# First loads on two DMA queues, and the layer norm of the first batches shared out among three engines, in a gated cross-attention kernel with an expert layer

## What is computed

```python
q = layernorm(x) @ Wq + bq                      # 8 x 256 x 256
k, v = ctx @ Wk + bk, ctx @ Wv + bv             # 8 x 120 x 256
x = x + tanh(g_xattn) * softmax(q @ k.T) / 16 @ v
h = layernorm(x)
e = argmax(h @ router_w.T)                      # one of 8 experts for each token
y = (silu(h @ gate_w[e].T) * (h @ up_w[e].T)) @ down_w[e].T   # inner width 704
out = x + tanh(g_ffn) * y
```

## Time and profile before

| | us |
|---|---|
| median of three runs | 236.29 |
| lowest and highest | 235.4, 236.63 |
| the profiled execution, its own time | 235.78 |
| its span in the profile | 233.9 |

### The profile page before, as it was taken

How to read it: one execution, slowest core, us unless ns; L and a number is a source line. 1 busy time by engine, 2 the same in 40 slices (tenths; PEclk the granted TensorE clock), 3 DMA queues, 4 the chain that set the end, 5 groups by cost and what they waited for, 6 DMA issues and landing times.

```text
span 233.9 us, 4473 instructions
## 1 busy us (share of the span) xinstructions
PE 199.9 (85%) x1187; PEld 171.1 (73%) x1187; DVE 132.8 (57%) x436; ACT 107.5 (46%) x217; POOL 133.0 (57%) x124
## 2 busy tenths in 40 slices
PE   0797699998774788999999999999999999999620
PEld 0655688896674667888887888888888887888510
DVE  0289689977669505636544636546546545556410
ACT  2233577776420145465339475267494304443200
POOL 3000009869273699329966989967989962331110
PEclk9999999999859559999999999999999999999985
DMA  4999211773910116641481093381011031110010
GB/s 83 369 382 383 98 48 46 245 271 116 372 36 0 55 38 244 213 152 45 144 326 28 1 353 115 137 323 49 1 49 44 1 93 24 49 46 4 1 45 0
DMA packets 11824, 29.41 MB, mean 126 GB/s; under 512 B 2222, under 2 KB 8241, under 8 KB 10770
## 3 DMA queue, kind: packets, MB, share of 16 engines
q1 hardware_dynamic: 6848, 21.70, 26.1%
q0 software_dynamic: 2064, 5.12, 7.3%
q10 hardware_dynamic: 2882, 2.24, 2.8%
HBM read 24.85 MB, written 4.72 MB: 126 GB/s over the span
## 4 chain that ended last, share of the span: by engine, by line
PE 72%; DVE 13%; issue 5%; DMA 4%; ACT 2%; SPq 1%; POOL 0%; ACTq 0%; POOLq 0%; DVEq 0%
PE ps L860 33%; PE ps L872 12%; PE ps L839 6%; PE ps L875 5%; DMA xin<-in_x 4%; PE ps L746 3%; PE ps L767 3%; DVE st L942 2%; PE ps L717 2%; PE ps L832 2%; PE ps L728 2%; PE ps L756 2%; PE ps L708 1%; PE ps L809 1%; DVE V L1067 1%
## 5 line engine op out<-in xcount | busy, mean ns | idle before, releaser
L860 PE MATMUL ps<-wgu,xhT 128*128 x360 | 83.2, 385 | 1.2 <-issue 1.2
L860 PEld LDWEIGHTS ps<-wgu,xhT 128*128 128x128 f32 x360 | 66.4, 192 | 12.4 <-issue 1.6
L872 PE MATMUL ps<-wd,hT 128*128 x120 | 42.9, 395 | 2.5 <-DVE hT L1112 2.4
L451 POOL DMA_INDIRECT xin<-x_rows,table x23 | 22.8, 990 | 31.7 <-DVE xin L1133 22.8
L386 POOL TENSOR_TENSOR wgu<-raw_gu,wgu (+1 forms) x12 | 38.6, 3252 | 0.1
L1120 DVE TENSOR_TENSOR A<-xin,ps 128x512 f32<-128x512 f32 (+1 forms) x40 | 20.5, 520 | 26.7 <-ACT xin L624 12.2
L409 POOL TENSOR_TENSOR wgu<-raw_gu,wgu 128x352 fp32r<-128x352 f32 x16 | 14.5, 945 | 34.7 <-ACT wgu L548 34.7
L624 ACT ACTIVATE xin<-ps 128x512 f32<-128x512 f32 (+1 forms) x40 | 18.4, 466 | 31.5 <-PE ps L860 27.8
L456 POOL DMA_INDIRECT out<-xin,table x20 | 20.3, 1016 | 19.7 <-DVE xin L1133 14.5
L618 ACT ACTIVATE hT<-ps 128x512 fp32r<-128x512 f32 x20 | 11.9, 593 | 35.3 <-PE ps L839 30.9
L875 PE MATMUL ps<-wd,hT 128*128 x100 | 28.0, 280 | 0.0
(11 more groups left out here) (148 smaller groups left out, 290.2 us busy)
## 6 DMA issues: line engine op xcount, KB each, us to landing
raw_gu<-in_Wgu SPq DMA_DIRECT2D x8, 1408.0 KB, 8.1
both<-in_Wd SPq DMA_DIRECT2D x8, 640.0 KB, 4.6
xin<-in_x SPq DMA_DIRECT2D x8, 256.0 KB, 8.0
x_rows<-x ACTq DMA_DIRECT2D x8, 256.0 KB, 4.2
both<-in_WdL SPq DMA_DIRECT2D x16, 64.0 KB, 4.7
both<-in_ctxT SPq DMA_DIRECT2D x1, 960.0 KB, 8.2
xin<-x_rows,table POOLq DMA_INDIRECT x23
out<-xin,table POOLq DMA_INDIRECT x20
```

The lines of the kernel that those rows point to most:

```text
L451: pool.indirect_dma_start(out=xg[:, j % SEATS, :], out_offset=None, in_=rows, in_offset=bass.IndirectOffsetOnAxis(ap=table[:, j:j + 1], ax ...
L860: last = pe.matmul(ps[:, g, 0:2 * WIDE if g < 2 else 4 * REST], xhT[:, j % 2, x_part, c, :], w, start=(c == 0 and (x_part, w_part) == (0, 0)),
L872: last = pe.matmul(ps[:, 6, 0:2 * H], hT[:, 0, c, :], wd[:, slot, c].rearrange("p o a n -> p (o a n)"), start=(c == 0), stop=(c == CI - 1) ...
```

## The change

The loads start on two queues: `wqT`, the context, the gates (each as one number to one partition) and the value bias on ScalarE's; `wkT`, x, `wv` and, after all of x, `wrT` on SyncE's. The gates are spread to 128 partitions by a one-row matmul with `mean_w` into bank 7, which Tanh reads with a scale of 256.

VectorE first fills a spare tile with ones, and TensorE multiplies it five times into bank 7 before it waits for the weights. The score weights fill banks 0, 1, 4, 5 in place of 0 to 3; halves 0 and 1 come before the transposes and context of batch 0, half 2 before its scores, half 3 after them. The router's mean product moves from before the transposes of batch 0 to just ahead of the loop.

VectorE takes the roots of batch 0 alone, then those of batches 1 to 3; GpSimd takes the Newton steps of batches 4 to 7 after a first guess on VectorE. ScalarE normalises batches 0 to 2, VectorE batches 3 to 7. The small blocks of `nwt` get columns of their own for each group. VectorE's measuring of batches 4 and 5 now stands before the minima of batch 0, that of 6 and 7 after them.

```diff
@@ sync
             sp.dma_start(wkT[:], ap(WkT, C)).then_inc(d_wq, 16)
-            sp.dma_start(wqT[:], ap(WqT, C)).then_inc(d_wq, 16)
-            sp.dma_start(ctx_sb, ap(ctxT, C)).then_inc(d_ctx, 16)
...
                 sp.dma_start(xin[:, TB * b:TB * b + TB, :], xv[b]).then_inc(d_x[b], 16)
+            sp.dma_start(wrT[:], ap(WrT, C)).then_inc(d_wr, 16)
@@ gpsimd
+            pool.wait_ge(v_guess1, 1)
+            newton(pool, link, mv1[:, AWAY, 0], rs1[:, AWAY], nm1[:, AWAY], AWAY).then_inc(p_st1, 1)
+
             for e in range(SPLIT - 1):
                 low_pieces(e)
@@ scalar
-            act.dma_start(gates[:, 0:1], g_x.to_broadcast([P, 1])).then_inc(d_g, 16)
-            act.dma_start(gates[:, 1:2], g_f.to_broadcast([P, 1])).then_inc(d_g, 16)
-            act.dma_start(bvb[:], bv.to_broadcast([P, H])).then_inc(d_sm, 16)
-            act.dma_start(wrT[:], WrT.rearrange("(c p) n -> p c n", c=C)).then_inc(d_sm, 16)
-            act.wait_ge(d_g, 32)
-            act.activation(tg[:], gates[:], ACT.Tanh).then_inc(a_tg, 1)
+            act.dma_start(wqT[:], WqT.rearrange("(c p) n -> p c n", c=C)).then_inc(d_wq, 16)
+            act.dma_start(ctx_sb, ctxT.rearrange("(c p) n -> p c n", c=C)).then_inc(d_ctx, 16)
+            act.dma_start(gates[0:1, 0:1], g_x).then_inc(d_g, 16)
+            act.dma_start(gates[0:1, 1:2], g_f).then_inc(d_g, 16)
+            act.dma_start(bvb[:], bv.to_broadcast([P, H])).then_inc(d_bv, 16)
...
+            def norm1(i):
+                act.wait_ge(v_st1, 1 if i == 0 else 2)
+                if i >= 2:
+                    act.wait_ge(t_t1, i - 1)
+                for k in range(TB):
+                    t = TB * i + k
+                    ins = act.activation(xn[:, i % 2, k, 0:H - 1], xin[:, t, 0:H - 1], ACT.Identity,
+                                         scale=rs1[:, t:t + 1], bias=nm1[:, t:t + 1])
+                ins.then_inc(a_xn, 1)
...
-            for q in range(4):
...
-            turned1(0)
-            turned1(1)
+            norm1(0)
+            act.wait_ge(t_tg, 1)
+            act.activation(tg[:], ps[:, 7, 0:2], ACT.Tanh, scale=float(H)).then_inc(a_tg, 1)
+            act.wait_ge(a_wqbk, 1)
+            scored(0)
+            scored(1)
+            turned1(0)
+            scored(2)
+            norm1(1)
             exps(0)
+            scored(3)
+            turned1(1)
+            norm1(2)
@@ tensor
+            pe.wait_ge(v_quiet, 1)
+            for _ in range(5):
+                pe.matmul(ps[:, 7, 0:2 * H], quiet[:, 0:P], quiet[:], start=True, stop=True)
             pe.wait_ge(d_wq, 32)
...
+            pe.wait_ge(d_g, 32)
+            pe.wait_ge(k_pool, 5)
+            pe.matmul(ps[:, 7, 0:2], mean_w[0:1, :], gates[0:1, :], start=True, stop=True).then_inc(t_tg, 1)
             pe.wait_ge(d_ctx, 16)
...
-            pe.wait_ge(a_a, 4)
+            score_weights(0)
+            score_weights(1)
+            pe.wait_ge(k_pool, 13)
+            pe.wait_ge(a_a, 1)
             turn1(0)
             pe.wait_ge(d_wv, 16)
             context(0)
+            score_weights(2)
+            pe.wait_ge(a_a, 2)
             scores(0)
+            score_weights(3)
             turn1(1)
+            router_mean()
             for i in range(B):
                 turn2(i)
@@ vector
+            dve.memset(quiet, 1.0).then_inc(v_quiet, 1)
             dve.wait_ge(d_wq, 32)
...
+            for t in HERE:
+                link(measured(t.start // TB, t.stop // TB))
+                link(moments(t))
+                scales(t)
+            dve.memset(oh[:, NTOK, :], 0.0)
+            dve.wait_ge(a_tg, 1)
+            link(dve.tensor_scalar(tgn[:], tg[:, 0:1], NORM, None, ALU.mult))
+            dve.wait_ge(d_bv, 16)
+            link(dve.tensor_scalar(bvt[:], bvb[:], tgn[:, 0:1], None, ALU.mult))
+            measured(OWN + 1, OWN + 3)
+            minima(0)
+            context(0)
+            link(measured(OWN + 3, B))
+            link(moments(AWAY))
+            guess(dve, link, mv1[:, AWAY, 1], AWAY).then_inc(v_guess1, 1)
+            dve.wait_ge(t_wr, 1)
...
             dve.wait_ge(k_pool, 13)
-            dve.memset(oh[:, NTOK, :], 0.0)
-            context(0)
-            minima(0)
-            scales(slice(2 * TB, NTOK))
-            norm1(2)
             for i in range(B + 1):
```

More of the change, by code:

```diff
@@ L517, in _, with scored @@
             act.activation(wqbk[:], ps[:, 6, 0:C], ACT.Copy, scale=-1.0).then_inc(a_wqbk, 1)
+            def norm1(i):
[7 more added lines that the diff above has]
+                ins.then_inc(a_xn, 1)
+            def scored(q):
+                n, m = q // 2, q % 2
+                act.wait_ge(t_a, q + 1)
+                act.activation(A[:, m, 480 * n:480 * n + 480], ps[:, A_BANK[q], 0:480], ACT.Identity, scale=-1.0,
+                               bias=wqbk[:, m:m + 1]).then_inc(a_a, 1)
             def turned1(i):
@@ L685, in _, with score_weights, router_mean @@
             last.then_inc(t_wqbk, 1)
+            pe.wait_ge(d_g, 32)
+            pe.wait_ge(k_pool, 5)
+            pe.matmul(ps[:, 7, 0:2], mean_w[0:1, :], gates[0:1, :], start=True, stop=True).then_inc(t_tg, 1)
             pe.wait_ge(d_ctx, 16)
-            pe.wait_ge(a_mt, C)
-            for q in range(4):
+            def score_weights(q):
                 n, m = q // 2, q % 2
+                if q == 3:
+                    pe.wait_ge(a_mt, C)
                 for c in range(C):
-                    last = pe.matmul(ps[:, q, 0:480], MT[:, c, P * m:P * m + P], ctx_sb[:, c, 480 * n:480 * n + 480],
+                    if q == 0:
+                        pe.wait_ge(a_mt, c + 1)
+                    last = pe.matmul(ps[:, A_BANK[q], 0:480], MT[:, c, P * m:P * m + P], ctx_sb[:, c, 480 * n:480 * n + 480],
                                      start=(c == 0), stop=(c == C - 1))
                 last.then_inc(t_a, 1)
[L695 to L700, removed]
+            def router_mean():
+                pe.wait_ge(d_wr, 16)
+                pe.wait_ge(a_a, 4)
+                for c in range(C):
+                    last = pe.matmul(ps[:, 5, 0:E], mean_w, wrT[:, c, :], start=(c == 0), stop=(c == C - 1))
+                last.then_inc(t_wr, 1)
             def turn1(i):
-                pe.wait_ge(v_xn, i + 1)
+                if i < OWN:
+                    pe.wait_ge(a_xn, i + 1)
+                else:
+                    pe.wait_ge(v_xn, i + 1 - OWN)
                 if i:
@@ L925, in norm1, with measured, moments @@
                 ins.then_inc(v_xn, 1)
+            def measured(lo, hi):
+                for b in range(lo, hi):
+                    dve.wait_ge(d_x[b], 16)
+                    for k in range(TB):
+                        ins = dve.bn_stats(st1[:, TB * b + k, :], xin[:, TB * b + k, :])
+                return ins
+            def moments(t):
+                for n in range(t.start, t.stop):
+                    ins = dve.bn_aggr(mv1[:, n, :], st1[:, n, :])
+                return ins
             def scales(t):
-                n = t.stop - t.start
-                link(guess(dve, link, mv1[:, t, 1], n))
-                newton_fused(dve, link, mv1[:, t, 0], rs1[:, t], nm1[:, t], n).then_inc(v_st1, 1)
+                link(guess(dve, link, mv1[:, t, 1], t))
+                newton_fused(dve, link, mv1[:, t, 0], rs1[:, t], nm1[:, t], t).then_inc(v_st1, 1)
+            dve.memset(quiet, 1.0).then_inc(v_quiet, 1)
             dve.wait_ge(d_wq, 32)
@@ L1005, in route @@
                 ins.then_inc(v_oh, 1)
-            dve.wait_ge(k_pool, 13)
-            dve.memset(oh[:, NTOK, :], 0.0)
-            context(0)
-            minima(0)
-            scales(slice(2 * TB, NTOK))
-            norm1(2)
+            dve.memset(oh[:, NTOK, :], 0.0)
[10 more added lines that the diff above has]
+            dve.wait_ge(t_wr, 1)
+            for c in range(C):
+                ins = dve.tensor_tensor(wrc[:, c, :], wrT[:, c, :], ps[:, 5, 0:E], ALU.subtract)
+            ins.then_inc(v_wrc, 1)
+            dve.wait_ge(k_pool, 13)
             for i in range(B + 1):
@@ L1026, in _ @@
             dve.wait_ge(v_aggr, B)
[L1027 removed]
+            guess(dve, link, mv2[:, :, 1], ALL).then_inc(v_guess, 1)
             route(B - 1)
```

70 lines of the change are left out of this document (25 added, 45 removed).

## The result

Four runs of the changed kernel have a median of 228.82 us (228.05 to 230.77), beside 236.44 us for the kernel before on the same chip: a ratio of 0.970, with an interval of 0.963 to 0.977. The profiled execution took 228.05 us with a span of 226.0. In two later comparisons, each on another chip, the same kernel came out at 0.989 (0.979 to 0.998) and 0.982 (0.974 to 0.991), so 0.970 is the largest gain of the three. All medians here are over every run of a kernel, and all ratios are over its fast runs alone, those within 1.5% of its fastest.

What follows compares the result with a forecast made beforehand. The opening, loads then VectorE's chain, was taken to bound the loop's start: 1.8 us from loads, 1.3 and 0.3 from the first two iterations, less 0.1, gave 3.3 us, from 236.29 to 233.0 us; range 231.5 to 235.8.

Steps and rivals of the forecast that it cites:

- The weights: First loads: with wkT and wqT on two queues the weights arrive at 5.1 us in place of 7.18.
- the weights don't come sooner: First loads: the 1028-byte rows may themselves be slow, so x(0) stays at 10.8 us; time 235.0, chance 0.30.
- x of batch 0: First loads: x shares the engines with the context, lands 3.6 us behind the weights, at 8.7 us in place of 10.8.
- the rival that follows from it: First loads: x of batch 0 comes well ahead of the context; 1.0 to 1.5 us more gained, 231.7, chance 0.10.
- VectorE's chain: Opening: VectorE's work from the arrival of x of batch 0 through the minima of batch 0, 11.37 us.
- the way to the loop: Opening: from the arrival of x of batch 0 to turn2(0), 13.5 us against 13.23 before.
- the first iteration: Batch loop: turn2(1) comes 3.4 us after turn2(0) in place of 4.7, saving 1.3 us.
- The 0.3 us of the second iteration: Batch loop: TensorE has 4.65 us of work in the 4.96 the second iteration takes; 0.3 us counted as saved.
- What comes later I take as moved with it.: From turn2(2) on, rest of loop, sort and experts: work unchanged, so all moves by as much as turn2(2), 3.3 us.
- The slower rival: Opening: TensorE at the lower of its two clocks, loop starting near 30 us; time 240.7 us, chance 0.07.
- Two of my signs of a wrong forecast: Opening: VectorE waiting for scores before the minima of batch 0; score-weight matmuls taking twice 0.40 us from start to start.

Runs made afterwards that it cites:

- the filled kernels: The kernel before and the changed kernel, each with added matmuls in the opening, at the loop's end and in the sort: 235.42 and 228.69 us.

## Why the prediction was wrong

- **The weights** (5.1 predicted, 4.7 measured). The arrival was near, the cause was not. I read 3.3% of the engines for ScalarE's queue as proof that its packets cost nothing. With the 4-byte packets the other queue moved 226 packets in 1.9 us, without them 497. The rival "the weights don't come sooner" fell. Its rule from the Trainium skill, DMA: Bandwidth & Descriptors, section "Issuing engines are not separate DMA queues", holds for the weights all the same: one queue brought them at 4.53 and two at 4.71.
- **x of batch 0** (3.6 us behind the weights predicted, 1.8 measured). This step failed: x did not come in with the context, it passed it. With the earlier weights it made x(0) land at 6.55 in place of 8.7. wkT was there 3.2 us after its issue and wqT 3.9 us, and x stands behind the first and the context behind the second; that this start was the cause is my reading. I had named 1.5 as the lower bound and given the rival that follows from it, with x(0) at 6.6, a chance of 0.10. I also priced it low, as if TensorE took over as bound; with an early clock VectorE stayed the bound, and x's whole 1.8 us reached turn2(0).
- **VectorE's chain** (11.37 predicted, 11.71 measured, 6.55 to 18.26, with a wait of 0.57 for x of batch 2 that I had at nothing; the six measurements at 4.03/12 are 2.0 and not 2.1), **the way to the loop** (13.5 predicted, 13.67) and **the first iteration** (3.4 predicted, 3.30) were right. The 0.3 us of the second iteration did not come: it takes 4.96 as before. With the measured x(0) the sum would have been 5.45 us at turn2(2), and the traces differ by 5.2.
- **"What comes later I take as moved with it."** This step failed too. Another 3.1 us (8.33 less 5.22) came between turn2(2) and the first expert tile. The 2.2 us of it in the sort are the clock's: the kernel without dummies has the changed kernel's program there and takes 2.1 us longer at 0.71, and the kernel before with throwaway matmuls takes 1.95 less at 0.98. The 0.9 us ahead of the sort go with a granted clock of 0.95 before and 1.00 after, and no run separates them further. In the repeats the clock took some of the gain back: ratios of 0.989 and 0.982 lie on either side of the forecast's 0.986, but that is luck: turn2(0) came 2.1 to 2.3 us later there than in the first profile, for a late clock.
- **The slower rival** named the right mechanism, though I took the full clock in the row of 11.9 to 18.4 from a column that says 1.00 in every opening; it is the pace, 16 matmuls in 6.5 us, that shows it. With a late rise turn2(0) came 2.1 to 3.3 us later than in the first profile, and not 7.8 (30 for 22.2), for the clock did rise before the third half. In no comparison did it make the changed kernel slower than the kernel before. Two of my signs of a wrong forecast, VectorE waiting for the scores and score weights at twice their 0.40 us, came in those executions and not in the first.
- The range left out gains of over 4.8 us, as its lower end took only the loads into account and no term for the clock.

What stays open: how much of the 6.7 us between the filled kernels is the clock's. In their profiles 1.1 us more come up to the sort, 0.6 are lost in it and 0.6 come after it, at granted clocks that are still not the same (0.91 and 0.86 in the sort). Open too is what the loads are worth in the old order under an early clock, and why the clock rises early in one execution and late in the next.

## What to carry to other kernels

A transfer that spreads one number over 128 partitions can slow every other load beside it, and one that spreads a row did so in one of two places here; where such a load is early, load it once and spread it with a matmul. A second queue paid here by letting an urgent load pass a large one, so look for who waits behind whom and less for bandwidth. And where a kernel's time depends on when TensorE's clock rises and falls, don't judge an order by one pair of executions: compare marks in several traces, with the granted clock and the pace of like matmuls beside each. Filling TensorE's gaps in both kernels did not make their clocks alike here.

## What the runs showed that I had not expected

- 130 packets of 4 bytes on one queue, 3.3% of the engines' time, held the other to 226 packets in 1.9 us; without them it moved 497.
- From the first sort matmul to the transposes of the first expert tile it takes 21.3 to 21.9 us in the six profiles where the 18 gate and up matmuls run in 4.1 us, and 23.5 us or more in the twelve where they take 5.7 us or more. Both groups have kernels of either order.
- The clock's rise in the opening differs between executions of one kernel: the first two score-weight halves took 3.49 us in one and 5.29 in another, with arrivals alike to 0.05 us. The five dummies, 2.3 us of work with a gap of 0.9 us behind them, changed nothing; eight that reached up to the weights brought full pace for the first product in three profiles of four.
- Executions of the kernel before spread over 5.8 us on one chip (231.04 to 236.83), more than the whole change was forecast to bring.
